# Latent attention of a macaron block: masked maxima on VectorE, scores by key tile, one query projection per pair, values in four runs

## Chip, cores and metric

One core of a Trainium2 chip runs the whole program. The metric is the device time of one execution in microseconds (us), the median of the runs. Engines: TensorE (PE for its matmuls, PEld for its weight loads), VectorE (DVE), ScalarE (ACT), GpSimd (POOL) and SyncE (SP), which here only issues DMAs.

## The reference

The program is a chain of six residual steps on x of shape (4, 1024, 128): a routed feed-forward step, an attention with a polynomial in place of softmax, the routed step again, a feed-forward step, the latent attention, and the feed-forward step again. The change touches only the latent attention:

```python
Wdkv = x @ latent_w + latent_b                       # (4, 1024, 36): keys and values of all heads
q = einsum('btc,hcl->bhtl', x, Wd_w) + Wd_b          # 16 heads of 36
scores = einsum('bhtl,bsl->bhts', q, Wdkv) / sqrt(8)
scores = where(causal, scores, -inf)
y = einsum('bhts,bsl->bhtl', softmax(scores), Wdkv)
out = y.transpose(0, 2, 1, 3).reshape(b, t, 16 * 36) @ out_w + out_b
```

## The kernel before

The latent attention is `attn1_phase`. It works batch by batch (4), and in each batch through 8 pairs of heads; pair m has the heads c = 0 and 1. Each engine has its own instruction stream, built from `start`, `pair` and `finish` by `pipeline`, and the streams meet at semaphores. A pair's work is spread over three rounds of the loop: in the round of pair m, TensorE computes the transposed scores and the values of pair m, the row maxima of pair m+1, and the query projection of pair m+2.

- **Queries.** `project(m, c)` multiplies the normalised input by the projection of head c. Precision is kept by splitting each float32 number into a high and a low part of type fp32r and adding three products, so it is three matmuls of 512 columns for each half sequence. The weights hold each head's 36 columns three times over, so that 108 rows come out; ScalarE (`low_query`, line 1795) and VectorE (`query`, line 1904) make rows high, high, low out of them and write them into qS.
- **Maxima.** `scores_max(m, q, v, keys)` takes tile v of 16 (head v // 8, query tile j = v % 8), multiplies 128 queries by the (j + 1) * 128 keys before them, and adds the causal mask of the last 128 columns by one more matmul of a bf16 identity and a bf16 mask (line 1642). VectorE's `maximum` takes the row maximum (line 1910). Two PSUM regions alternate, so tile v waits for the maximum of tile v - 2. `transpose_max`, `high_max` and `low_max` turn the 16 columns of maxima into rows, and four DMAs (`maxima` on SP, lines 1536 and 1537) put them into rows 108 and 109 of qS, where they are subtracted inside the score product.
- **Transposed scores.** `scores(m, q, u)` works through ten units: per half sequence a diagonal unit of four tiles of 128 x 128 and a mask matmul of 512 columns (line 1659), a unit of 384 and 128 columns, one of 256, and for the second half four full units of 512. Unit u of a head waits until ScalarE's exponential (line 1820) has read unit u - 1 from the same PSUM bank. The exponentials go to probs, which has two slots.
- **Values.** `values(m, q, u)` (line 1671) multiplies probs by V in plain float32. Head 0 goes to partitions 0 to 63 and head 1 to partitions 64 to 127, so these matmuls use half-width tiles of the array. The values of unit u - 1 follow the scores of unit u.
- **What goes where.** `MAXIMA` says how many maxima tiles follow the scores of each unit: all 16 are spread over units 0 to 6. After unit 8 comes `transpose_max`, after that the projection of head 0 of pair m+2, after unit 9 that of head 1. Pair 6 of a batch also opens the next batch (`opens`), and after pair 7 comes `finish`, the output product.

Of the kernel before, what the change touches and what calls it, by code (L numbers as in the profile page):

```python
# [34 lines left out]
def after(n):  # L35

    return n + 1 + LEAD
# [1378 lines left out]
PAIRS = HEADS // 2  # L1416
STACK = 3 * LAT
KROWS = STACK + 2
ZW = 5 * P
VW = 64  # L1420
L1_COLS = 2 * LAT + 8 + 4 * HEADS


def key_units(s):
# [6 lines left out]
    return [diagonal, split, half] + [[(i, 0, 0, HALF, False)] for i in range(k)]  # L1431


def attn1_phase(nc, t, tag):
# [8 lines left out]
    with ExitStack() as ctx:  # L1443
        def sb(name, shape, dt=F32):
# [5 lines left out]
        wd = [sb(f"wd{i}", [P, HEADS * STACK], F32R) for i in range(2)]  # L1450
        lat = [sb(f"lat{i}", [P, STACK], F32R) for i in range(2)]
        v_bias, k_bias, k_low, q_low = cols[:, 0:LAT], cols[0:STACK, 36:37], cols[0:STACK, 37:38], cols[0:STACK, 38:39]
        q_bias = cols[0:STACK, 40:40 + HEADS]
        k_lbias = sb("k_lbias", [STACK, 1])
        qb_low = sb("qb_low", [STACK, HEADS])
# [8 lines left out]
        wcur = sb("wcur", [P, 2, 2 * STACK], F32R)  # L1464
        bcur = sb("bcur", [STACK, 2, 2])
        qT = sb("qT", [STACK, 2, HALF], F32R)
# [4 lines left out]
        probs = sb("probs", [P, 2, 2, HALF])  # L1471
# [3 lines left out]
        zT = sb("zT", [P, 2, ZW])  # L1475
        res = ResidualAdd(ctx, nc, sem, t, tag, 1)
# [5 lines left out]

        k_in, w_high, w_low, rstd_ready = sem("k_in"), sem("w_high"), sem("w_low"), sem("rstd_ready")
        minus = sb("minus", [2, SEQ], F32R)
        const_ready, minus_ready = sem("const_ready"), sem("minus_ready")
# [3 lines left out]
        wq_ready, qp_ready, qt_ready, qs_ready = sem("wq_ready"), sem("qp_ready"), sem("qt_ready"), sem("qs_ready")  # L1489
        sm_ready, mx_ready, mt_ready, mh_ready, ml_ready, m_in = (  # L1490
            sem("sm_ready"), sem("mx_ready"), sem("mt_ready"), sem("mh_ready"), sem("ml_ready"), sem("m_in"))
        s_ready, p_ready, pv_ready, y_ready, yc_ready = (
            sem("s_ready"), sem("p_ready"), sem("pv_ready"), sem("y_ready"), sem("yc_ready"))
# [4 lines left out]
        units = [(s, u) for s in range(2) for u in key_units(s)]  # L1498
        NU = len(units)
        NQ0 = len(key_units(0))  # L1500
        PRODUCTS = ((0, 0), (1, 0), (0, 1))

        def pipeline(eng, start, pair, finish):


            def element(b, more):
                with eng.Fori(0, PAIRS // 2 - 1) as i:
                    for q in range(2):
                        pair(b * PAIRS + i * 2 + q, q, i * 2 + q, b, (True, True))
# [14 lines left out]
        MAXIMA = (range(0, 4), range(4, 6), range(6, 7), range(7, 9), range(9, 12), range(12, 14), range(14, 16))  # L1524

        with nc.Block() as block:
            @block.sync
            def _(sp):
# [9 lines left out]

                def pair(m, q, i, b, ahead):
                    if ahead[0]:  # L1540
                        maxima(m + 1, 1 - q)

                pipeline(sp, lambda: maxima(0, 0), pair, lambda b, more: None)
# [536 lines left out]
```

## Time and profile before

| | |
|---|---|
| median of 3 runs | 3431.35 us (3430.93 to 3438.45) |
| span of the profiled execution | 3431.1 us |
| PE, DVE, ACT busy over the span | 89%, 66%, 38% |
| latent attention, from and to | about 2280 us to 3325 us |
| one pair in the steady part | 26.3 to 27.0 us |
| all four batches, 32 pairs | about 1045 us |

The profiled execution's own time is its span. A busy share counts an instruction from its first to its last cycle, also while the next one already runs. The column of the granted clock tells at which of its two levels, 1.2 and 2.4 GHz, TensorE ran: 1.00 is 2.4 GHz.

### The profile page before, as it was taken

The numbers are of one execution on the slowest core, as the hardware profiler recorded it, in microseconds if no ns is written. First come the engines' busy times: TensorE is split into PE (matmuls) and PEld (weight loads), VectorE is DVE, ScalarE is ACT, GpSimd is POOL, SyncE is SP. The second block draws the span as 40 slices with busy tenths as digits, with TensorE's granted clock in tenths as the row PEclk, the third lists the DMA queues.
The fourth block names the chain that finished last, engine by engine and source line by source line (L and its number), as shares of the span: only waits on it lengthen the run. The fifth ranks groups of instructions, "written<-read, shape, count | busy, mean of one in ns | idle before, by whom it ended". The sixth has DMA issues, their size and how long they took to land. (4 is left out here: it accounts for less than half of the span.)

```text
span 3431.1 us, 60614 instructions
## 1 busy us (share of the span) xinstructions
PE 3037.7 (89%) x18088; PEld 2189.2 (64%) x18088; DVE 2268.8 (66%) x5128; ACT 1317.9 (38%) x2660; POOL 765.6 (22%) x1073
## 2 busy tenths in 40 slices
PE   5999999787777877769999999779989989999987
PEld 4777777565555555547777777446666666666653
DVE  6777777587786877857777777345555555555533
ACT  2111111266665765641111111225545545545532
POOL 1323232154354444422323232000000000000000
PEclk9999999888998888979999999779999999999998
DMA  3000000000000000011000000000000000000000
GB/s 121 0 0 0 0 0 0 1 2 2 3 3 3 2 2 2 2 63 35 0 0 0 0 0 0 1 0 1 1 2 1 1 2 1 1 2 1 1 1 25
DMA packets 13037, 24.17 MB, mean 7 GB/s; under 512 B 2306, under 2 KB 7682, under 8 KB 12804
## 3 DMA queue, kind: packets, MB, share of 16 engines
q1 hardware_dynamic: 12804, 21.22, 1.9%
q8 instruction: 127, 2.08, 0.3%
q14 instruction: 106, 0.87, 0.1%
HBM read 18.52 MB, written 2.10 MB: 6 GB/s over the span
## 5 line engine op out<-in xcount | busy, mean ns | idle before, releaser
L555 DVE SCALAR_TENSOR_TENSOR moe_acc<-moe_ps,moe_comb,moe_acc 128x512 f32<-128x512 f32 x896 | 661.7, 745 | 174.0 <-PE moe_ps L304 170.9
L1335 DVE SCALAR_TENSOR_TENSOR attn_R<-attn_R 128x512 f32<-128x512 f32 (+1 forms) x592 | 478.5, 864 | 115.5 <-ACT attn_R L1221 115.1
L1910 DVE TENSOR_REDUCE attn_mx<-attn_psm 128x1 f32<-128x128 f32 (+7 forms) x512 | 369.3, 754 | 243.0 <-PE attn_psm L1642 242.4
L1820 ACT ACTIVATE attn_probs<-attn_pse 128x512 f32<-128x512 f32 (+1 forms) x640 | 323.4, 553 | 330.1 <-PE attn_pse L1655 263.6
L304 PE MATMUL moe_ps<-moe_Wg,moe_xh 128*128 128x512 f32 x1024 | 328.8, 403 | 24.2 <-DVE moe_Wu L501 24.2
L1221 ACT ACTIVATE attn_R<-attn_ps 128x512 f32<-128x512 f32 (+1 forms) x640 | 321.2, 568 | 64.9 <-PE attn_ps L1079 64.8
L335 PE MATMUL moe_ps<-moe_Wd,moe_ih 128*128 128x512 f32 x1024 | 338.0, 411 | 0.0
L304 PE MATMUL moe_ps<-moe_Wu,moe_xh 128*128 128x512 f32 x1024 | 337.1, 411 | 0.0
L1671 PE MATMUL attn_psy<-attn_probs,attn_V 128*64 128x128 f32 (+3 forms) x2304 | 317.7, 397 | 0.1
L1079 PE MATMUL attn_ps<-attn_qS,attn_kM 128*128 128x128 f32 (+3 forms) x1152 | 263.9, 372 | 45.9 <-issue 43.2
L1079 PEld LDWEIGHTS attn_ps<-attn_qS,attn_kM 128*128 128x128 f32 x1152 | 210.1, 228 | 109.9 <-issue 60.0
L1655 PE MATMUL attn_pse<-attn_qS,attn_kS 110*128 110x128 f32 (+3 forms) x1152 | 261.2, 341 | 13.0 <-issue 9.7
L1098 PE MATMUL attn_ps<-attn_R,attn_KV 128*32 128x128 f32 (+3 forms) x2304 | 171.4, 412 | 110.3 <-DVE attn_R L1335 110.2
L454 POOL TENSOR_SCALAR moe_part<-consts,moe_pick,moe_prob 128x8 f32<-128x8 f32 x256 | 98.2, 398 | 755.8 <-ACT moe_prob L389 755.8
L1655 PEld LDWEIGHTS attn_pse<-attn_qS,attn_kS 110*128 110x128 f32 x1152 | 172.7, 194 | 121.3 <-issue 83.4
L1023 POOL TENSOR_TENSOR attn_L<-attn_L,attn_small 128x512 f32<-128x512 f32 x128 | 206.7, 1646 | 163.5 <-ACT attn_L L1220 163.5
L304 PEld LDWEIGHTS moe_ps<-moe_Wg,moe_xh 128*128 128x128 f32 x1024 | 194.5, 191 | 73.9 <-issue 28.0
L1639 PE MATMUL attn_psm<-attn_kS,attn_qS 108*128 108x512 f32 (+3 forms) x672 | 212.0, 402 | 14.3 <-DVE attn_mx L1910 10.7
L388 ACT ACTIVATE moe_prob<-moe_gap 128x2 f32<-128x2 f32 x64 | 13.1, 204 | 548.6 <-DVE moe_gap L546 548.6
L335 PEld LDWEIGHTS moe_ps<-moe_Wd,moe_ih 128*128 128x128 f32 x1024 | 186.0, 191 | 41.7 <-issue 1.1
L304 PEld LDWEIGHTS moe_ps<-moe_Wu,moe_xh 128*128 128x128 f32 x1024 | 187.2, 192 | 36.8
L1561 POOL CAST attn_wcur<-attn_wd 128x216 fp32r (+1 forms) x64 | 21.5, 365 | 828.8 <-DVE attn_qS L1904 822.9
(207 smaller groups left out, 5302.4 us busy)
## 6 DMA issues: line engine op xcount, KB each, us to landing
moe_stageg<-in_w_gate SPq DMA_DIRECT2D x8, 512.0 KB, 6.8
moe_stageu<-in_w_up SPq DMA_DIRECT2D x8, 512.0 KB, 7.5
moe_stageg<-in_w_down SPq DMA_DIRECT2D x8, 512.0 KB, 3.6
out<-X SPq DMA_DIRECT2D x1, 2048.0 KB, 8.7
attn_qS<-attn_mh SPq DMA_DIRECT2D x64, 4.0 KB
attn_qS<-attn_ml SPq DMA_DIRECT2D x64, 4.0 KB
attn_wd<-in_wd SPq DMA_DIRECT2D x1, 864.0 KB, 5.5
attn_w<-in_wqkv SPq DMA_DIRECT2D x1, 768.0 KB, 5.1
```

Source lines behind the costliest of these rows:

```text
L304: last = pe.matmul(expert_bank[j % 4][:, :], a[q][:, :], w[b][:, cols], start=k == 0, stop=k == 2)
L335: last = pe.matmul(y_bank[h][:, :], a[q][:, rows], W[2][b][:, cols], start=c == 0 and k == 0, stop=c == KC - 1 and k == 2)
L555: dve.scalar_tensor_tensor(acc[:, q, r, :], expert_bank[j % 4][:, :], comb[:, q, r, e:e + 1], acc[:, q, r, :], ALU.mult, ALU.add).then_inc ...
L1023: pool.tensor_tensor(L[:, s, j, :], L[:, s, j, :], seen, ALU.mult).then_inc(g_ready, 1)
L1079: last = pe.matmul(e_bank[j][:, at_:at_ + n], kM[q][:, j, kt * P:(kt + 1) * P], qS[q][:, s * HALF + qc:s * HALF + qc + n], start=not diago ...
L1221: act.activation(R[:, u % 2, j, HALF - n:HALF], e_bank[j][:, HALF - n:HALF], ACT.Relu).then_inc(r_ready, 1)
L1335: dve.scalar_tensor_tensor(r, r, -SLOPE, r, ALU.add, ALU.mult).then_inc(u_ready, 1)
L1639: pe.matmul(m_all[:, base + lo:base + hi], qS[q][c][0:STACK, j * P:(j + 1) * P], keys[0:STACK, lo:hi], start=True, stop=hi < (j + 1) * P)
L1655: last = pe.matmul(e_bank[c][:, at_:at_ + n], kS[:, kt * P:(kt + 1) * P], qS[q][c][:, s * HALF + qc:s * HALF + qc + n], start=True if not ...
L1671: last = pe.matmul(y_bank[VW * c:VW * (c + 1), qc:qc + n], V[:, kt, :], probs[:, u % 2, c, at_:at_ + n], start=first and k == 0, stop=end, ...
L1820: act.activation(probs[:, u % 2, c, HALF - n:HALF], e_bank[c][:, HALF - n:HALF], ACT.Exp, scale=SCORE_SCALE).then_inc(p_ready, 1)
L1910: dve.reduce_max(mx[:, q, v:v + 1], m_all[:, base:base + (v % 8 + 1) * P], AX.X).then_inc(mx_ready, 1)
```

## The change

Four things change in the latent attention.

- **Masked maxima.** The mask matmul of each maxima tile goes. VectorE holds a float32 tile `causal` (896 zeros and the mask) and uses one `tensor_tensor_reduce` in place of `reduce_max`: it adds `causal` to the scores, writes the sum to `masked` and the maximum to mx. Before it stands a wait on the tile before the last.
- **Scores by key tile.** The diagonal units are cut by key tile: 512 columns with a mask of 128, 384 and 128 columns with a mask of 256, 256 columns with a mask of 128.
- **One projection.** `project(m)` computes both heads at once, 72 rows, six matmuls a pair. ScalarE makes the high part qh, VectorE the low part ql, and SP copies the rows to their places in qS by six DMAs of 36 rows x 4 KB (`query_rows`). The maxima of that pair wait for these DMAs. They are issued behind the four DMAs of `maxima`.
- **Four runs of values.** probs has five slots, and the values of a pair come in four runs: units 0 to 2 after unit 3, units 3 to 5 after unit 6, units 6 and 7 after unit 8, and units 8 and 9 after unit 0 of the next pair. MAXIMA moves with them: none at unit 0, three in a row at units 2, 4, 5 and 7, the last at unit 7. The first two pairs of a batch are written out before the loop.

```diff
+RING = 5
+PAIR = 2 * LAT
+def tile_units(s):
+    k = 4 * s
+    return [[(k, 0, 0, HALF, True)], [(k + 1, P, P, 3 * P, True), (k + 3, 0, 3 * P, P, True)],
+            [(k + 2, 2 * P, 2 * P, 2 * P, True)]] + [[(i, 0, 0, HALF, False)] for i in range(k)]
...
-        probs = sb("probs", [P, 2, 2, HALF])
+        probs = sb("probs", [P, RING, 2, HALF])
+        causal = sb("causal", [P, SEQ])
+        masked = sb("masked", [P, 2, SEQ])
+        TOGETHER = ((0, 1, 2), (3, 4, 5), (6, 7), (8, 9))
+        AFTER = {3: 0, 6: 1, 8: 2}
...
-        MAXIMA = (range(0, 4), range(4, 6), range(6, 7), range(7, 9), range(9, 12), range(12, 14), range(14, 16))
+        MAXIMA = ((), range(0, 2), range(2, 5), range(5, 6), range(6, 9), range(9, 12), range(12, 13), range(13, 16))
...
+                def query_rows(m, q):
+                    sp.wait_ge(ql_ready, after(m * 2 + 1))
+                    sp.wait_ge(s_ready, after((m - 1) * 2 * NU - 1))
+                    for c in range(2):
+                        for k, part in enumerate((qh, qh, ql)):
+                            sp.dma_start(f32(qS[q][c][k * LAT:(k + 1) * LAT, :]),
+                                         f32(part[c * LAT:(c + 1) * LAT, :])).then_inc(q_in, 16)
...
-                def project(m, c):
+                def project(m):
...
-                            last = pe.matmul(m_bank[2 * c + s][0:STACK, :], wcur[:, w, c * STACK:(c + 1) * STACK],
+                            last = pe.matmul(m_bank[s][0:PAIR, :], wcur[:, w, :],
                                              xT[a][:, s * HALF:(s + 1) * HALF], start=k == 0, stop=k == 2)
...
                 def scores_max(m, q, v, keys):
+                    if v == 0:
+                        pe.wait_ge(q_in, (m + 1) * ROWS_IN)
...
-                    pe.matmul(m_all[:, base + j * P:base + (j + 1) * P], t.identb, t.neg_qk, start=False, stop=True).then_inc(sm_ready, 1)
...
                     for u in range(NU):
                         scores(m, q, u)
+                        if u == 0 and not first_pair:
+                            values(m - 1, NG - 1)
...
-                        if u >= 1:
-                            values(m, q, u - 1)
+                        if u in AFTER:
+                            values(m, AFTER[u])
...
+                def high_query(m):
+                    for s in range(2):
+                        act.wait_ge(qp_ready, after(m * 2 + s))
+                        if s == 0 and not (isinstance(m, int) and m == 0):
+                            act.wait_ge(q_in, m * ROWS_IN)
+                        act.activation(qh[:, s * HALF:(s + 1) * HALF], m_bank[s][0:PAIR, :], ACT.Identity,
+                                       bias=bcur[:, :]).then_inc(qh_ready, 1)
...
+                def low_query(m):
+                    for s in range(2):
+                        half = slice(s * HALF, (s + 1) * HALF)
+                        dve.wait_ge(qh_ready, after(m * 2 + s))
+                        dve.scalar_tensor_tensor(ql[:, half], m_bank[s][0:PAIR, :], bcur[:, :], f32(qh[:, half]),
+                                                 ALU.add, ALU.subtract).then_inc(ql_ready, 1)
...
                     dve.wait_ge(sm_ready, after(m * 16 + v))
-                    base = (v % 2) * 2 * HALF
-                    dve.reduce_max(mx[:, q, v:v + 1], m_all[:, base:base + (v % 8 + 1) * P], AX.X).then_inc(mx_ready, 1)
+                    dve.wait_ge(mx_ready, after(m * 16 + v - 2))
+                    dve.sem_inc(max_pause, 1)
+                    base, n = (v % 2) * 2 * HALF, (v % 8 + 1) * P
+                    dve.tensor_tensor_reduce(masked[:, v % 2, 0:n], m_all[:, base:base + n], causal[:, SEQ - n:SEQ], 1.0, NEG,
+                                             ALU.add, ALU.max, mx[:, q, v:v + 1]).then_inc(mx_ready, 1)
```

## Rows read from the trace of the kernel before

**Rows 1.** The page, busy time by engine and the granted clock in 40 slices

```profile
PE 3037.7 (89%) x18088; PEld 2189.2 (64%) x18088; DVE 2268.8 (66%) x5128; ACT 1317.9 (38%) x2660; POOL 765.6 (22%) x1073
...
PEclk9999999888998888979999999779999999999998
```

**Rows 2.** Busy time by stretch: us, PE, PEld, DVE, ACT, POOL, clock, DMA, GB/s

```profile
12.00:14.00 2.00, 0.00 (x0) 0.00 (x0) 1.84 (x10) 0.00 (x0) 0.00 (x0) 1.00 1.03 410
2302.00:2306.00 4.00, 2.76 (x13) 1.78 (x14) 3.40 (x7) 0.00 (x0) 2.27 (x6) 1.00 0.01 2
2306.00:2310.00 4.00, 2.61 (x13) 1.43 (x12) 3.65 (x6) 0.00 (x0) 0.00 (x0) 0.99 0.00 0
2310.00:2314.00 4.00, 3.96 (x12) 2.36 (x13) 2.98 (x5) 0.00 (x0) 0.00 (x0) 0.50 0.00 0
2321.00:2530.00 209.00, 204.09 (x1303) 128.67 (x1302) 116.76 (x176) 111.55 (x211) 7.39 (x32) 1.00 0.00 1
```

**Rows 3.** SP's timeline, a first load, and first DMAs of `maxima` in two pairs

```profile
8.41 0.43 SPq L267 DMA_DIRECT2D moe_stageg<-in_w_gate  x1
...
2344.06 0.64 SPq L1536 DMA_DIRECT2D attn_qS<-attn_mh  x1
2344.75 0.64 SPq L1537 DMA_DIRECT2D attn_qS<-attn_ml  x1
...
2477.41 0.63 SPq L1536 DMA_DIRECT2D attn_qS<-attn_mh  x1
```

**Rows 4.** Groups by line and shape in the latent attention, mean ns behind busy us

```profile
L1910 DVE TENSOR_REDUCE attn_mx<-attn_psm 128x1 f32<-128x1024 f32 x64 | 78.1, 1220 | 60.0 <-PE attn_psm L1642 60.0
L1910 DVE TENSOR_REDUCE attn_mx<-attn_psm 128x1 f32<-128x512 f32 x64 | 44.0, 687 | 7.6 <-PE attn_psm L1642 7.3
L1904 DVE SCALAR_TENSOR_TENSOR attn_qS<-attn_psm,attn_bcur,attn_qT 108x512 fp32r<-108x512 f32 x128 | 91.1, 749 | 76.0 <-PE attn_pse L1655 46.5 <-ACT attn_qT L1795 29.3
L1876 DVE TENSOR_TENSOR attn_xT<-attn_psm,attn_xT 128x512 fp32r<-128x512 f32 x8 | 5.2, 688 | 1.7 <-ACT attn_xT L1774 1.6
L1335 DVE SCALAR_TENSOR_TENSOR attn_R<-attn_R 128x512 f32<-128x512 f32 x464 | 433.3, 989 | 115.5 <-ACT attn_R L1221 115.1
L1795 ACT ACTIVATE attn_qT<-attn_psm,attn_bcur,attn_small 108x512 fp32r<-108x512 f32 x122 | 89.6, 785 | 40.7 <-PE attn_psm L1626 40.2 <-DVE attn_qS L1904 0.5
L1820 ACT ACTIVATE attn_probs<-attn_pse 128x512 f32<-128x512 f32 x512 | 281.2, 596 | 215.4 <-PE attn_pse L1655 148.9 <-PE attn_pse L1659 63.9
```

**Rows 5.** Timeline of a steady pair: weight loads and matmuls where kinds of work meet

```profile
2396.90 1.20 PEld L1626 LDWEIGHTS attn_psm<-attn_xT,attn_wcur 128*108 128x108 f32 x6 [0.81 <-issue]
2398.15 0.42 PEld L1655 LDWEIGHTS attn_pse<-attn_qS,attn_kS 110*128 110x128 f32 x2
...
2402.19 0.52 PEld L1655 LDWEIGHTS attn_pse<-attn_qS,attn_kS 110*128 110x128 f32 x4 [0.81 <-issue]
2403.33 0.20 PEld L1639 LDWEIGHTS attn_psm<-attn_kS,attn_qS 108*128 108x128 f32 x1
...
2420.06 0.72 PE L1655 MATMUL attn_pse<-attn_qS,attn_kS 110*128 110x512 f32 x2
2420.67 1.08 ACT L1820 ACTIVATE attn_probs<-attn_pse 128x512 f32<-128x512 f32 x2 [1.22 <-PE attn_pse L1655]
2420.71 1.08 PE L1671 MATMUL attn_psy<-attn_probs,attn_V 128*64 128x512 f32 x4
2421.72 0.73 PE L1655 MATMUL attn_pse<-attn_qS,attn_kS 110*128 110x512 f32 x2
```

**Rows 6.** Timeline of the last batch: the last DMA of `maxima` and who waits

```profile
3266.22 0.64 SPq L1537 DMA_DIRECT2D attn_qS<-attn_ml  x1
...
3268.03 0.66 PE L1655 MATMUL attn_pse<-attn_qS,attn_kS 110*128 110x128 f32 x4 [1.42 <-DMA attn_qS<-attn_ml]
```

**Rows 7.** Timeline of the end of one steady pair, from maxima to row DMAs

```profile
2422.29 0.27 PE L1647 MATMUL attn_pso<-consts,attn_mx 128*16 128x128 f32 x1
...
2423.59 0.28 DVE L1914 TENSOR_TENSOR attn_ml<-attn_pso,attn_mh 16x128 fp32r<-16x128 f32 x1 [2.37 <-ACT attn_mh L1800]
```

More of the change, by code:

```diff
@@ L1496, in attn1_phase @@
         kc_ready, act_pause, pool_pause = sem("kc_ready"), sem("act_pause"), sem("pool_pause")
-        units = [(s, u) for s in range(2) for u in key_units(s)]
+        units = [(s, u) for s in range(2) for u in tile_units(s)]
         NU = len(units)
-        NQ0 = len(key_units(0))
+        NQ0 = len(tile_units(0))
         PRODUCTS = ((0, 0), (1, 0), (0, 1))
@@ L1506, in element @@
             def element(b, more):
-                with eng.Fori(0, PAIRS // 2 - 1) as i:
+                for i in range(2):
+                    pair(b * PAIRS + i, i, i, b, (True, True))
+                with eng.Fori(1, PAIRS // 2 - 1) as i:
                     for q in range(2):
@@ L1541, in pair @@
                         maxima(m + 1, 1 - q)
-                pipeline(sp, lambda: maxima(0, 0), pair, lambda b, more: None)
+                    if ahead[1]:
+                        query_rows(m + 2, q)
+                pipeline(sp, start, pair, lambda b, more: None)
             @block.gpsimd
@@ L1655, in scores @@
                             last = pe.matmul(e_bank[c][:, at_:at_ + n], kS[:, kt * P:(kt + 1) * P],
-                                             qS[q][c][:, s * HALF + qc:s * HALF + qc + n], start=True if not diagonal else k == 0,
+                                             qS[q][c][:, s * HALF + qc:s * HALF + qc + n], start=k == 0,
                                              stop=not diagonal, skip_group_check=diagonal)
                         if diagonal:
-                            last = pe.matmul(e_bank[c][:, :], t.identb, t.neg_kq, start=False, stop=True, skip_group_check=True)
+                            lo, hi = min(p[1] for p in pieces), max(p[1] for p in pieces) + P
@@ L1677, in start @@
                     latents(0)
+                    pe.wait_ge(xl_ready, after(1))
+                    project(0)
                     latent_rows(0)
-                    for c in range(2):
-                        project(0, c)
                     for v in range(16):
@@ L1891, in start @@
                     next_keys(0)
-                    for g in range(4):
-                        query(0, 0, g)
+                    low_query(0)
                     for v in range(16):
@@ L1929, in pair @@
                     if ahead[1]:
-                        for g in range(4):
-                            query(m + 2, q, g)
+                        low_query(m + 2)
                 def finish(b, more):
```

159 lines of the change are left out of this document (76 added, 83 removed).

## The prediction

> **What bounds the kernel now.** I read the page first: TensorE is the busiest engine of the whole program [rows 1]. The change touches only the latent attention, so the next view is the busy time by stretch. In 2321 to 2530 us TensorE shows 204.09 of 209 us at a granted clock of 1.00, VectorE 117 and ScalarE 112 [rows 2]. The reader is to see that the other two are a little over half full, and that nothing is said yet of whether their work lies in the right place. SP's timeline gives the length of a pair: from 2344.06 to 2477.41 are five pairs, 26.67 us each [rows 3]. Then the groups for the price of one operation [rows 4], and the timeline for what happens where two kinds of work meet [rows 5, 6, 7].
>
> **Prices.** Six projection matmuls of 512 columns take 1.25 us from first to next load, so 512 fp32r columns cost 0.21 us, one column a cycle at 2.4 GHz. Four tiles of 128 columns need four weight loads in 0.52 us: a load that nothing hides costs 0.125. Values: the scores of one unit start at 2420.06 (load 0.125, stream 0.43, end 2420.61), the values at 2420.71, the next scores load at 2421.72. From 2420.61 to that unit's first column at 2421.85 are 1.24 us, of which the four value matmuls stream 4 x 0.213 = 0.85. So going into half-width tiles and out again costs 0.38 us [rows 5]. VectorE's maximum costs 154 ns and 1.04 ns a column (687 at 512, 1220 at 1024); successive ones are taken to overlap by 0.07 [rows 4]. Two exponentials take 1.08 us [rows 5].
>
> **TensorE's savings, per pair.**
> - 16 mask matmuls of the maxima: 128 columns (0.053) and the 0.072 us of the next weight load that so short a matmul doesn't hide, 0.125 each: 2.0 us.
> - Projection, 12 matmuls to 6: 6 x 0.213 = 1.3 us.
> - Values: nine runs become four (the last two units already lie together), 5 x 0.36 (0.38 less a little that the masks beside them share): 1.8 us. Their columns stay the same.
> - Scores by key tile: a diagonal unit took 1.14 us (2402.19 to 2403.33) and now takes two times 512 + 128 columns with one open load, about 0.63. The 384/128 unit gains a mask of 256 columns a head and the 256 unit one of 128, with loads in part hidden: 0.12 and 0.2 us. Net 0.2 a half sequence, 0.4 us a pair.
>
> Sum 5.5 us. If TensorE's own work were all, a pair would fall by a fifth, and 27 to 30 such pairs by some 160 us.
>
> **Why I don't book that.** I laid both orders out by hand over a pair: each engine's instructions in program order, each as early as the prices and its waits allow. For the kernel before this gives 24.9 us of TensorE work and 1.2 us of waits, 26.1 us a pair against 26.67 measured; its landmarks stay close to the trace (unit 7 starts 17.7 us behind unit 0 and unit 8 19.3; in the trace 2420.06 - 2402.19 = 17.9 and 19.5 [rows 5]). The new order gives 19.3 us of work and 9.7 us of waits, 29.05 us a pair. The waits, in the pair's time (unit 0 at 0):
>
> 1. *Rows of the queries, 2.4 us.* The copies start only when the projection has passed through ScalarE and VectorE. Unit 8's `transpose_max` is visible at 24.2; then values of units 6 and 7 (to 26.1) and the projection (to 27.4); ScalarE makes two high halves (0.69 each: 785 ns with bias and scale pointers before, 596 for an exponential without them, the middle taken), VectorE the second low half (749 ns [rows 4]): low rows ready at 29.3. SP then issues six DMAs at 0.675 us each (2344.06 to 2344.75 [rows 3]). A DMA of 4 KB was awaited until 1.81 us after its issue began [rows 6]; 147 KB at the 410 GB/s of the first loads [rows 2] adds 0.4 to 0.5, so I take 2.3. The last row lands 0.675 x 5 + 2.3 = 5.7 us later, at 35.0, which is 5.9 us into the next pair. There, unit 0's scores, the held-over values (2.1 us) and unit 1's scores are through by 3.5, and maxima tile 0 stands in front of everything else in TensorE's queue. SP's four DMAs of `maxima` (issued 24.9 to 27.6) are past by then and don't delay the six.
> 2. *Maxima three in a row, 4.3 us.* Only two regions exist, so the third of each group waits for VectorE to finish the first: 0.9 at tiles 2 to 4, 2.4 at tiles 8 to 11, 1.0 at tile 15. Between the groups VectorE has nothing, because TensorE is in 2.1 us of values. Before, the maxima started at unit 0 with a value run of 1 us between groups, and these waits were 1.2 us.
> 3. *`transpose_max`, 1.4 us.* The last maximum (1.22 us) now follows unit 7, and only unit 8's scores cover it. Before, it followed unit 6 with a value run and two units of scores behind it.
> 4. *Unit 0 of the next pair, 1.6 us.* It needs unit 9's exponential, which stands in ScalarE's queue behind the two high halves, and these wait for the projection. Before, the values of units 8 and 9 filled this place.
>
> The four DMAs of the maxima rows (ml in [rows 7], then 4 x 0.675 + 1.8) land at about 28.7, just ahead of unit 0: if ScalarE were quicker, this wait would take over.
>
> So a pair costs 29.05 - 26.1 = 2.95 us more.
>
> **Bounds of what the trace doesn't show.** *The masked maximum:* a TENSOR_TENSOR from PSUM costs 688 ns at 512 columns, the reduction 687 [rows 4], so I take it at the same price. Above stands line 1335's 989 ns at 512, 0.3 us more, which gives 31.6 us a pair. Below, at half a cycle a column, 26.6; nothing in PSUM-reading float32 rows goes that fast. *The copies:* an issue of 0.43 us, as for a large load early in the program [rows 3], gives 27.8; copies that land before anyone needs them 27.4; a landing of 3.6 us 30.35. So no end of the copies' price brings the pair under 26.1.
>
> A rule of the Trainium skill speaks on the masked maximum: the page Vector Engine (DVE) Microarchitecture Reference, section Points that are easy to get wrong, says that such an instruction with two SBUF sources wider than bf16 and an accumulator runs at half its rate. Here one source lies in PSUM, so by its words it doesn't apply; if it did, rival C below would be the forecast. No row of before shows a fused maximum.
>
> **Sum over the run.** Twenty steady intervals (pairs 1 to 5 of four batches): +59. Pair 0 of each batch has neither held-over values nor a wait for rows (they were copied before `finish`): 29.05 - 2.4 - 2.1 = 24.6, -1.5 x 4 = -6. The opening pairs save two value runs and six matmuls behind unit 8 but wait longer for rows: +1 x 3. The last pair of three batches ends with its values behind the late exponential: +6.7 x 3 = +20. In the last batch pair 6 keeps waits 1 to 3 (+2), pair 7 has only scores and values (-2). The start trades one projection for six DMAs: 0. The smaller weight copies save 1 to 2, the mask tile gives 1 back. Together +75 on the profiled execution's 3431.1; the median is 3431.35, so **about 3506 us**.
>
> **The rivals.**
> - *A, faster: the chain between two pairs is covered.* Waits 1, 3 and 4 (5.4 us) form one chain from the last maximum to the next pair's first. If it ran beside TensorE's work, only the waits for VectorE would stay: 23.7 us, 2.4 less than 26.1, over 27 pairs -65: 3366 us. It decides from 3 us of that chain gone. For it: 5.5 us of work truly goes, and VectorE and ScalarE have room. Against: each link is in queue order in the code. Chance 0.17.
> - *B, TensorE's clock.* At the start of the phase, with maxima alone, TensorE was busy 2.76 and 2.61 of 4 us, and the clock then went from 1.00 to 0.50 [rows 2]. In the new order the stretch from 3.5 to 10 us of each pair has 2.4 + 0.9 us of waits in 6.5, a similar share. If the clock falls there, the value run of 2.1 us takes 4.2; over 27 pairs some 60 to 75 us more, 3565 to 3580. Chance 0.2.
> - *C, the masked maximum runs at half rate.* Twice the columns' time gives 35.0 us a pair, +5.9 x 27 = +160 on the forecast: 3665 us. With 0.3 us more an instruction, +2.6 x 27 = +70: 3576. Chance 0.08 for both, mostly the latter.
> - *D, no change:* the waits come to the 5.5 us that the work loses. Chance 0.05.
> - The forecast itself, 3440 to 3560 (its lower end is the quick issue, 1.2 us a pair less; its upper end the slow landing and a little of B): 0.5.
>
> **Numbers.** Within 0.3% (10 us) is what a measurement can't tell from no change. Faster 0.17, same 0.05, slower 0.78. The range is 3405 to 3640: it leaves out the lower half of A and the far end of C.
>
> **What would show it.** Right: SP's first maxima DMA comes every 29 us in the steady part; line 1642 is gone; TensorE's idle time names the row DMAs at the first maxima tile (2.4 us a pair), the masked maximum at the third of a group, and the last maximum before `transpose_max`; its busy share in the steady part falls from 98% to some 75%. Wrong: if the rows land before 3.5 us into the pair, step 1 goes; if six row DMAs issue in under 0.5 us each, half of it; if the masked maximum shows much above 1.22 us at 1024 columns, C; if the granted clock shows under 1.00 in steady pairs, B; if a steady pair is under 26 us, the whole layout of waits was wrong, and A is right.

## The result and the profile after

The changed kernel takes 3754.4 us (median of 4 runs, 3751.3 to 3760.9) against 3431.1 before. The ratio is 1.0939, 95% interval 1.0918 to 1.0961. The profiled execution has a span of 3749.5 us. So it is 323 us slower. I had forecast 75 us slower, and a range that ended at 3640.

The page, busy time and granted clock; they answer to [rows 1].

```profile
PE 3079.9 (82%) x16488; PEld 2117.4 (56%) x16488; DVE 2232.1 (60%) x5577; ACT 1264.7 (34%) x2590; POOL 754.2 (20%) x1041
...
PEclk9999999799888898799999986878887878798888
```

TensorE has 1600 matmuls fewer, and is busy 42 us longer. A matmul's duration grows at the lower clock, and the last 16 slices of the clock show mostly 7 and 8 where there were nearly all nines. The busy time by stretch says the same of the steady part [rows 2]; below it are stretches of 2 us of one pair.

```profile
2321.00:2530.00 209.00, 156.61 (x628) 81.23 (x627) 72.35 (x190) 70.81 (x138) 3.35 (x18) 0.79 0.09 26
```

```profile
2400.00:2402.00 2.00, 1.63 (x10) 0.71 (x6) 0.00 (x0) 1.04 (x3) 0.00 (x0) 1.00 0.58 158
2402.00:2404.00 2.00, 0.00 (x0) 0.00 (x0) 0.00 (x0) 0.54 (x2) 0.00 (x0) 1.00 0.48 141
2404.00:2406.00 2.00, 0.00 (x0) 0.00 (x0) 0.00 (x0) 0.00 (x0) 0.00 (x0) 0.72 0.28 98
2406.00:2408.00 2.00, 1.91 (x8) 1.72 (x8) 0.73 (x4) 0.67 (x2) 0.00 (x0) 0.50 0.00 0
...
2412.00:2414.00 2.00, 2.00 (x6) 0.63 (x8) 0.97 (x2) 0.00 (x0) 0.00 (x0) 0.50 0.00 0
2414.00:2416.00 2.00, 2.00 (x13) 0.95 (x10) 0.00 (x0) 0.00 (x0) 0.00 (x0) 0.72 0.00 0
...
2426.00:2428.00 2.00, 1.21 (x4) 0.67 (x4) 2.00 (x5) 0.32 (x1) 0.00 (x0) 1.00 0.00 0
2428.00:2430.00 2.00, 1.09 (x3) 0.38 (x5) 1.06 (x3) 1.03 (x3) 0.00 (x0) 0.69 0.00 0
2430.00:2432.00 2.00, 2.00 (x8) 0.47 (x4) 0.00 (x0) 0.00 (x0) 0.00 (x0) 0.50 0.02 4
```

For 4 us, 2402 to 2406, TensorE does nothing while the DMA moves 141 and 98 GB/s. The clock falls to 0.50 (1.2 GHz) within that wait (0.72 in its last 2 us) and stays there for some 9 us of the work behind it. It falls a second time between 2428 and 2430, in the second of two thin stretches (TensorE busy 1.21 and 1.09 of 2 us). SP's timeline shows why TensorE stands still [rows 3].

```profile
2392.25 0.66 SPq L1556 DMA_DIRECT2D attn_qS<-attn_mh  x1
...
2398.20 1.52 SPq L1565 DMA_DIRECT2D attn_qS<-attn_qh  x2
2399.76 0.71 SPq L1565 DMA_DIRECT2D attn_qS<-attn_ql  x1
2400.52 2.32 SPq L1565 DMA_DIRECT2D attn_qS<-attn_qh  x2
2402.89 0.71 SPq L1565 DMA_DIRECT2D attn_qS<-attn_ql  x1
2429.93 0.66 SPq L1556 DMA_DIRECT2D attn_qS<-attn_mh  x1
```

A pair lasts 2429.93 - 2392.25 = 37.7 us; it was 26.67, and I had laid out 29.05. The row copies begin at 2398.20, the last one at 2402.89. TensorE's timeline of the same pair (in brackets the idle time before, and who ended it), with one row of VectorE:

```profile
2406.09 0.79 PE L1676 MATMUL attn_psm<-attn_kS,attn_qS 108*128 108x128 f32 x2 [4.46 <-DMA attn_qS<-attn_ql]
...
2411.86 3.97 PE L1710 MATMUL attn_psy<-attn_probs,attn_V 128*64 128x512 f32 x16
...
2418.53 0.33 PE L1676 MATMUL attn_psm<-attn_kS,attn_qS 108*128 108x128 f32 x1 [0.91 <-DVE attn_mx L1949]
...
2421.96 2.37 PE L1710 MATMUL attn_psy<-attn_probs,attn_V 128*64 128x512 f32 x16
...
2428.91 0.38 PE L1683 MATMUL attn_pso<-consts,attn_mx 128*16 128x128 f32 x1 [1.11 <-DVE attn_mx L1949]
2429.22 3.39 PE L1710 MATMUL attn_psy<-attn_probs,attn_V 128*64 128x512 f32 x8
...
2435.42 0.50 PE L1691 MATMUL attn_pse<-attn_qS,attn_kS 110*128 110x512 f32 x1 [0.80 <-ACT attn_probs L1856]
```

```profile
2417.38 1.09 DVE L1949 CUSTOM_DVE_ANT_0 attn_masked<-attn_psm,attn_causal 128x896 f32<-128x896 f32 x1 [4.26 <-PE attn_psm L1676]
```

Sixteen value matmuls of the same shapes take 3.97 us mostly at the half clock and 2.37 at the full one. While they run TensorE makes no new tile: VectorE finishes the one that stood ready and is then idle for 4.26 us. And the groups by shape, beside [rows 4]:

```profile
L1949 DVE CUSTOM_DVE_ANT_0 attn_masked<-attn_psm,attn_causal 128x1024 f32<-128x1024 f32 x10 | 12.2, 1222 | 0.0
...
L1949 DVE CUSTOM_DVE_ANT_0 attn_masked<-attn_psm,attn_causal 128x512 f32<-128x512 f32 x11 | 7.6, 690 | 1.5 <-PE attn_psm L1676 1.5
L1949 DVE DVE_READ_ACCUMULATOR2_ANT attn_mx<- 128x1 f32 x86 | 7.2, 83 | 0.0
```

The masked maximum costs what the reduction did (1222 and 690 ns against 1220 and 687), but each drags a second instruction of 83 ns behind it.

### The profile page after: what moved, and what is told of

The parts are those of the page before. It is cut to its first block and busy times, and to the rows that moved or that the text cites. A ratio compares the mean times of both kernels' runs of the same rounds, so it can differ in the third digit from the quotient of the medians.

```text
span 3749.5 us, 57897 instructions
## 1 busy us (share of the span) xinstructions
PE 3079.9 (82%) x16488; PEld 2117.4 (56%) x16488; DVE 2232.1 (60%) x5577; ACT 1264.7 (34%) x2590; POOL 754.2 (20%) x1041
## 5 line engine op out<-in xcount | busy, mean ns | idle before, releaser
L1949 DVE CUSTOM_DVE_ANT_0 attn_masked<-attn_psm,attn_causal 128x128 f32<-128x128 f32 (+7 forms) x512 | 375.7, 757 | 608.7 <-PE attn_psm L1676 603.8
L1676 PE MATMUL attn_psm<-attn_kS,attn_qS 108*128 108x512 f32 (+3 forms) x672 | 241.3, 454 | 194.7 <-DMA attn_qS<-attn_ql 108.0
L1710 PE MATMUL attn_psy<-attn_probs,attn_V 128*64 128x512 f32 (+3 forms) x1536 | 370.9, 630 | 0.8 <-ACT attn_probs L1856 0.8
L1691 PE MATMUL attn_pse<-attn_qS,attn_kS 110*128 110x512 f32 (+3 forms) x768 | 269.2, 430 | 38.3 <-ACT attn_probs L1856 25.4
L1676 PEld LDWEIGHTS attn_psm<-attn_kS,attn_qS 108*128 108x128 f32 x672 | 140.7, 235 | 258.2 <-DVE attn_mx L1949 135.9
L1597 POOL CAST attn_wcur<-attn_wd 128x72 fp32r<-128x72 f32 (+1 forms) x64 | 13.9, 247 | 1096.3 <-DVE attn_ql L1941 1090.5
L1691 PEld LDWEIGHTS attn_pse<-attn_qS,attn_kS 110*128 110x128 f32 x768 | 156.4, 221 | 119.5 <-issue 70.0
L1710 PEld LDWEIGHTS attn_psy<-attn_probs,attn_V 128*64 128x64 f32 x1536 | 119.0, 172 | 184.4 <-issue 151.5
```

The lines of the kernel that those rows point to most:

```text
L1676: last = pe.matmul(m_all[:, base + lo:base + hi], qS[q][c][0:STACK, j * P:(j + 1) * P], keys[0:STACK, lo:hi], start=True, stop=True)
L1691: last = pe.matmul(e_bank[c][:, at_:at_ + n], kS[:, kt * P:(kt + 1) * P], qS[q][c][:, s * HALF + qc:s * HALF + qc + n], start=k == 0, stop ...
L1710: last = pe.matmul(y_bank[VW * c:VW * (c + 1), qc:qc + n], V[:, kt, :], probs[:, u % RING, c, at_:at_ + n], start=first and k == 0, stop=e ...
L1949: dve.tensor_tensor_reduce(masked[:, v % 2, 0:n], m_all[:, base:base + n], causal[:, SEQ - n:SEQ], 1.0, NEG, ALU.add, ALU.max, mx[:, q, v: ...
```

## The experiments

Each run is given as a ratio to the kernel before, measured beside it; "+130 us" is (ratio - 1) x 3431. First, which part of the change costs, put together and taken apart.

**e1: the change with the projection of before** (two heads' projections, rows straight into qS, no row copies).

```diff
-                    for c in range(2):
-                        for k, part in enumerate((qh, qh, ql)):
-                            sp.dma_start(f32(qS[q][c][k * LAT:(k + 1) * LAT, :]), ...
+                for c in range(2):
+                    project(m, c)
```

> The changed kernel with the projection of before (12 matmuls a pair, rows written by ScalarE and VectorE, no row DMAs); masked maxima, key tiles, four runs and the new MAXIMA stay. Theory R (the wait for the row DMAs and the fall of the clock that follows it cost most of the 11 us a pair): no TensorE idle of over 2 us, granted clock near 1.00 in steady pairs, a pair of 27.5 to 29 us, 3450 to 3500 us. Rival V (the waits for VectorE between three maxima in a row and the long value runs thin TensorE's work out and bring the clock down by themselves): the clock still falls in each pair, 31 us a pair or more, over 3560 us.

3564.5 us, ratio 1.0378 (1.0349 to 1.0407), +130. It fits neither range: 192 us go with the new projection, and 130 stay. In its trace the clock still falls up to twice a pair, among the maxima and value runs, with no row copies there:

```profile
2394.00:2396.00 2.00, 2.00 (x6) 0.64 (x7) 0.97 (x2) 0.50 (x1) 0.00 (x0) 0.50 0.00 0
...
2404.00:2406.00 2.00, 2.00 (x6) 0.65 (x7) 0.89 (x4) 0.69 (x2) 0.00 (x0) 0.50 0.00 0
```

The pair around these two stretches lasts 33.3 us, the one before it, whose clock falls only at its very end, 28.6. So the late order loses the clock by itself, here 4.7 us in a pair.

**e3: the new projection alone** on the kernel before: `project(m)`, `high_query`, `low_query`, `query_rows`, and nothing else.

> The kernel before with the new projection and its row DMAs alone. Theory R: the first maxima stand right behind unit 0's scores here, so TensorE waits some 4 us a pair for the rows, the clock falls behind it, and 1.3 us of matmuls are saved: a pair of 32 to 35 us, 3580 to 3680 us. Rival V: the row wait costs only itself, 29 to 30 us a pair, 3500 to 3530 us.

3647.9 us, ratio 1.0620 (1.0591 to 1.0649), +213. Its waiting tile, with the clock of the same stretch:

```profile
2396.23 0.47 PE L1660 MATMUL attn_psm<-attn_kS,attn_qS 108*128 108x128 f32 x1 [5.14 <-DMA attn_qS<-attn_ql]
```

```profile
2391.00:2393.00 2.00, 0.09 (x1) 0.00 (x0) 0.00 (x0) 1.94 (x3) 0.00 (x0) 0.98 0.58 158
2393.00:2395.00 2.00, 0.00 (x0) 0.00 (x0) 0.00 (x0) 0.00 (x0) 0.00 (x0) 0.50 0.51 162
...
2401.00:2403.00 2.00, 2.00 (x19) 1.72 (x17) 1.39 (x2) 0.00 (x0) 0.00 (x0) 0.50 0.00 0
```

TensorE waits for the row copies 29 times in this kernel, 160.6 us in total. One part of four, tried alone, costs two thirds of the whole loss.

**e4: the masked maxima alone** on the kernel before.

```diff
-                    dve.reduce_max(mx[:, q, v:v + 1], m_all[:, base:base + (v % 8 + 1) * P], AX.X).then_inc(mx_ready, 1)
+                    dve.tensor_tensor_reduce(masked[:, v % 2, 0:n], m_all[:, base:base + n], causal[:, SEQ - n:SEQ], 1.0, NEG,
+                                             ALU.add, ALU.max, mx[:, q, v:v + 1]).then_inc(mx_ready, 1)
```

> The kernel before with the masked maxima alone. TensorE loses 16 mask matmuls a pair (2.0 us by the hand layout), VectorE gains 0.08 us an instruction (1.3 us), and it is no bound here: a pair of 24.9 to 25.7 us, 3385 to 3410 us under both theories. If the mask matmuls were hidden anyway: 3431 us.

3438.3 us, ratio 1.0014 (0.9999 to 1.0030). The 2 us a pair that TensorE was spared bring nothing, though I had expected 3385 to 3410 us under both theories. The run changes two things at once: VectorE also has the 16 accumulator reads more.

**e5 and e6: masks and key tiles, in the early and in the late order of the maxima.** e5 adds `tile_units` to e4; e6 is e5 with one line more:

```diff
-        MAXIMA = (range(0, 4), range(4, 6), range(6, 7), range(7, 9), range(9, 12), range(12, 14), range(14, 16))
+        MAXIMA = ((), range(0, 2), range(2, 5), range(5, 6), range(6, 9), range(9, 12), range(12, 13), range(13, 16))
```

> The kernel before with the masked maxima and the transposed scores by key tile, and nothing else of the change: ten value runs a pair, the order of the maxima of before, the old projection. TensorE has 2.4 us a pair less to do (16 masks of 0.125 and 0.4 of the scores). If TensorE's own work sets the pair, 32 pairs give 3355 to 3385 us. If the chain from one maximum to the next sets it (a maximum, the accumulator read of 0.08 us behind it, the next scores), both savings only lengthen TensorE's waits: 3425 to 3445 us.

> As the last one, with the order of the maxima of after (none behind unit 0, three in a row behind units 2, 4, 5 and 7), still ten value runs a pair. Theory O (the late order with three in a row thins TensorE's work, and the granted clock falls): 3500 to 3570 us, near the 3564 of the kernel that has this order, the four runs and the old projection. Theory G (the grouped value runs starve the chain of maxima, since only two tiles of scores can stand ready, and the order alone costs a wait of 0.5 to 1 us a pair): 3430 to 3470 us, with a clock above 0.93.

e5: 3424.6 us, ratio 0.9963 (0.9945 to 0.9980), -13, as the chain of maxima would have it. e6: 3525.2 us, ratio 1.0243 (1.0219 to 1.0266), +83. The order alone costs 96 us, with ten value runs a pair. Theory O is right, and G, that the order hurts only through joined runs, falls. But under the late order joining them costs too: e1, the same with four runs, stands at 1.0378, 46 us above e6. Three neighbouring pairs of e6 with the same instructions:

```profile
2347.11:2375.42 28.31, 25.00 (x122) 12.75 (x121) 14.92 (x37) 13.81 (x27) 0.92 (x4) 1.00 0.01 2
2375.42:2417.04 41.62, 37.89 (x122) 18.54 (x121) 14.93 (x37) 15.70 (x28) 0.92 (x4) 0.63 0.00 0
2417.04:2445.67 28.63, 25.26 (x122) 12.98 (x121) 14.92 (x37) 13.82 (x27) 0.92 (x4) 1.00 0.00 1
```

The late order has two prices. At the full clock e6's pairs alternate in three of the four batches between some 28.5 and 30.1 us, where e5's last mostly 26.0 and 26.5: about 3 us a pair. And in this execution two pairs last 41.6 and the change to the last batch 71.7 in place of 61.6, with the clock down; beside pairs of 30.1 that is some 33 us. So about a third of the 96 us is the clock, and most of the rest is waiting.

**e7: the change with the projection and the order of before** (masked maxima, key tiles, four value runs).

> Masked maxima, key tiles and four value runs, with the order of the maxima of before and the old projection. Theory G: a value run of 2 to 3 us leaves VectorE idle for 1 to 2 us four times a pair, so the order does not save it: 3500 to 3580 us. Theory O: with the early order the five restarts of 0.36 us that the grouping spares come through at least in part: 3370 to 3430 us.

3426.9 us, ratio 0.9973 (0.9961 to 0.9984), -9. With the early order the four runs do no harm, and no good either (e5 is the same with ten runs; the intervals overlap). A steady pair lasts 26.9 us, no less than the 26.67 of before. One of its value runs, and VectorE's next maximum:

```profile
2407.31 2.37 PE L1690 MATMUL attn_psy<-attn_probs,attn_V 128*64 128x512 f32 x16
```

```profile
2410.95 0.42 DVE L1938 CUSTOM_DVE_ANT_0 attn_masked<-attn_psm,attn_causal 128x256 f32<-128x256 f32 x1 [2.41 <-PE attn_psm L1656]
```

**e11: the whole change in the early order** (the `MAXIMA` line of before).

> The whole change with the order of the maxima of before (four tiles behind unit 0). The late order cost 137 us with the old projection (3564 against 3427). If it costs as much under the new one: 3600 to 3640 us, below the 3648 of the new projection alone. If the rows' wait, which comes at the same instant of the pair in both orders, absorbs part of it, since the later tiles have nothing to wait for before the rows are there: 3660 to 3700. If the early tiles hold up the scores of unit 1 and with them the whole pair: 3740 or more.

3633.3 us, ratio 1.0579 (1.0540 to 1.0618), +199. This closes the square: -9 with neither cost (e7), +130 with the late order (e1), +199 with the new projection (e11), +322 with both. The projection and its copies cost 208 us in one order and 192 in the other; the order costs 139 under one projection and 123 under the other. They nearly add up. The projection's share can be set against the row waits of the changed kernel's trace:

```profile
PE attn_psm L1676 <- DMA attn_qS<-attn_ql: 132.1, 29, 9.7
```

(Us in total, how many waits, the longest one.) 132 of some 200 us are the waits themselves; e2 below speaks on the rest.

**What the row copies cost.** Four variants of the changed kernel.

*e8*: the copies of head 0 and head 1 are counted on two semaphores, and the first eight tiles wait for the first alone.

```diff
-                    if v == 0:
-                        pe.wait_ge(q_in, (m + 1) * ROWS_IN)
+                    if j == 0:
+                        pe.wait_ge(q_in[c], (m + 1) * ROWS_IN)
```

> The kernel after, with the six row copies counted on two semaphores, so that the first eight tiles of maxima wait for the three copies of the first head alone. The last of those three is issued about 3.1 us ahead of the last of the six, so the first tile of maxima starts some 3 us earlier in each pair. If the rows' wait costs what it lasts: 3 us by 30 pairs, 3750 less 90, 3650 to 3675 us. If it also costs TensorE its clock in the stretch behind it, and the shorter wait (2 us in place of 5) keeps it up: 3580 to 3640. If the second head's maxima then find their rows late, which they should not, since they come some 8 us later, no gain: 3740 or more.

3689.4 us, ratio 1.0729 (1.0702 to 1.0757), 72 less than the change. From the first copy's issue to tile 0 it is 2403.66 - 2397.78 = 5.9 us, 2.0 less than in the changed kernel (2406.09 - 2398.20 = 7.9) and not 3: the second head's copies follow on the same queue, and head 0's last one was there only 4.3 us after its issue began. None of the three expectations holds: the wait shrinks by less than 3 us, and the clock still falls in the pair.

*e9*: six copies of half the columns (the edit below, with n = 512). *e10*: twelve of half the columns, two for each of the six.

```diff
-                            sp.dma_start(f32(qS[q][c][k * LAT:(k + 1) * LAT, :]),
-                                         f32(part[c * LAT:(c + 1) * LAT, :])).then_inc(q_in, 16)
+                            sp.dma_start(f32(qS[q][c][k * LAT:(k + 1) * LAT, 0:n]),
+                                         f32(part[c * LAT:(c + 1) * LAT, 0:n])).then_inc(q_in, 16)
```

> The kernel after with six row copies of half the queries each (columns 0 to 511, from the third pair on; the other half keeps the rows of an older pair, so the scores of those queries are not this pair's). The number of copies and their order on the queue stay. Theory N (the number of copies sets when the last one lands: six issues of 0.77 us and a fixed time behind them): no change, 3735 to 3770 us. Theory S (their size sets it: 0.86 MB a pair at 160 GB/s is 5.4 us, which is what passes from the first issue's end to the wait's end): half the bytes take 2 to 2.7 us less a pair, 60 to 80 us less, and what the clock then gives back comes on top: 3640 to 3695 us.

> The kernel after with the same bytes in twelve copies of half the columns. Theory N: six more issues of 0.7 us a pair, 4.2 us by 30 pairs on the path, 3860 to 3900 us. Theory S: the queue keeps the bytes flowing at the same rate while it issues; 12 issues of 0.7 are 8.4 us, longer than the 5.4 us of the bytes, so the issues now decide and half of the 4.2 us shows: 3800 to 3850 us. Unchanged (3740 to 3770) if a small copy's issue is much cheaper than 0.7 us.

e9: 3704.8 us, ratio 1.0780 (1.0741 to 1.0819), 54 less than the change. e10: 3845.6 us, ratio 1.1189 (1.1149 to 1.1230), 86 more. e9's copies and its tile 0:

```profile
2399.63 1.52 SPq L1566 DMA_DIRECT2D attn_qS<-attn_qh  x2
2401.19 0.71 SPq L1566 DMA_DIRECT2D attn_qS<-attn_ql  x1
2401.94 1.47 SPq L1566 DMA_DIRECT2D attn_qS<-attn_qh  x2
2403.46 0.71 SPq L1566 DMA_DIRECT2D attn_qS<-attn_ql  x1
```

```profile
2405.85 0.79 PE L1677 MATMUL attn_psm<-attn_kS,attn_qS 108*128 108x128 f32 x2 [2.77 <-DMA attn_qS<-attn_ql]
```

Half-size copies issue every 0.77 us (3.83 from the first to the last) and the last is there 2.39 us later: 6.2 us. At full size one issue of the six is held up, 2.32 for two where e9 has 1.47, so that first to last takes 4.69, and the last needs 3.20: 7.9 us. So five steps from issue to issue make 3.8 us, the arrival of a half-size copy 2.4, and the second half of the bytes 1.7; what the first half's bytes take isn't shown apart. In e10 a first copy is issued at 2413.93 and tile 0 starts at 2424.70, 10.8 us, 4.6 more than in e9 for six more issues. So the count of copies is the larger part, and the size is real, but here smaller than the 2 us of theory S. e9 fell between the two theories. e10 fell into the range of theory S, which had the issues decide once there are twelve; but the 5.4 us that S puts between the first issue's end and the wait's end are some 7.1.

The waits for rows over the whole execution, for e9, e8 and e10:

```profile
PE attn_psm L1677 <- DMA attn_qS<-attn_ql: 91.4, 29, 9.8
PE attn_psm L1676 <- DMA attn_qS<-attn_ql: 77.7, 29, 7.8
PE attn_psm L1678 <- DMA attn_qS<-attn_ql: 223.0, 29, 12.6
```

Against 132.1 in the changed kernel, e9 waits 41 us less and is 54 faster, e8 54 less and 72 faster, e10 91 more and 86 slower. A shorter wait gave back somewhat more than its length, a longer one cost no more than its length.

*e2*: ahead of the wait for the rows, 36 matmuls of 256 columns that feed nothing.

```diff
+                            if u == WARM_AT and not last_pair:
+                                for _ in range(36):
+                                    pe.matmul(o_bank[:, 256:512], t.identb, t.neg_kq[:, 0:256], start=True, stop=True)
```

> The changed kernel with 36 matmuls of 256 columns (3.8 us at full clock) whose result nobody reads, put after unit 1's scores, in front of the wait for the row DMAs, in pairs 0 to 6 of each batch. Theory R: they lie inside a wait of 4.5 us, so they delay nothing where the rows are late, and keep the clock at 1.00 behind it: the maxima and value run behind the wait lose some 4 us, a pair goes from 37.7 to some 33.5 us, about 3640 us. Rival V: the clock falls a little later all the same; the time stays within 1% of 3754 us or rises.

3693.0 us, ratio 1.0740 (1.0708 to 1.0771), 68 less than the change, with more work. Tile 0 starts just as late behind the first copy (2402.92 - 2395.14 = 7.8 us), so what is won isn't the wait but the clock behind it: at least 68 us of the rows' price. The clock is held up only for a while, as rival V had it:

```profile
2403.00:2405.00 2.00, 1.79 (x8) 1.00 (x8) 1.20 (x5) 0.66 (x2) 0.00 (x0) 1.00 0.03 8
...
2407.00:2409.00 2.00, 2.00 (x6) 0.62 (x7) 0.97 (x2) 0.48 (x1) 0.00 (x0) 0.50 0.00 0
...
2417.00:2419.00 2.00, 2.00 (x7) 0.68 (x7) 0.91 (x4) 0.71 (x2) 0.00 (x0) 0.50 0.00 0
```

Behind tile 0 it shows 1.00, and then it falls twice, as in e1, where there is no such wait. So the time lies between theory R's 3640 us and rival V's 3716.

**e12: the late order (e6) with fillers** of 256 columns, four or five ahead of the third tile of each group of three.

```diff
+FILL = {4: 4, 8: 4, 11: 5, 15: 5}
...
+                                for _ in range(FILL.get(v, 0)):
+                                    pe.matmul(o_bank[:, 256:512], t.identb, t.neg_kq[:, 0:256], start=True, stop=True)
```

> The kernel with masked maxima, key tiles and the late order (3525 us), with 18 matmuls of 256 columns a pair that feed nothing, four or five ahead of the third tile of each group of three, where TensorE waits 0.6 to 0.9 us for VectorE. They last about 0.5 us a place at 2.4 GHz, so the waits cover them. If TensorE's thin stretches are what lowers the granted clock, it stays at 1.00 and each pair lasts 28.6 us, as the pairs at full clock do there: 3480 to 3500 us. If the clock falls for another reason, 3525 us and more, since at half clock the fillers are longer than the waits.

3504.9 us, ratio 1.0198 (1.0161 to 1.0236), against 1.0243 for e6. The intervals of the two ratios overlap a little, though the times don't (3502 to 3509 and 3513 to 3531). The pair that lasted 41.6 us in e6:

```profile
2376.55:2407.78 31.23, 28.59 (x141) 15.17 (x140) 14.93 (x37) 15.29 (x28) 0.92 (x4) 0.95 0.00 1
```

It lasts 31.2 us at 0.95. The time is just above the range of the first theory (3480 to 3500): no pair of 41.6 is left, but every second pair of most batches lasts 31.2 to 32.7 where e6 has 30.1. That speaks for the thin stretches as a cause of the clock's fall.

**Where TensorE's savings went.** e7 has all of the masks', key tiles' and four runs' savings, 4.2 us a pair by my count, and gains 0.3 (9 us by 32). Three variants of e7.

*e13*: each maximum over the first half of its columns, and the exponential's scale divided by 1024. *e14*: the mask matmul and the plain reduction of before. *e15*: only the last two groups of values joined.

```diff
+                    lo, n = SEQ - n, n // 2
-                                             scale=SCORE_SCALE).then_inc(p_ready, 1)
+                                             scale=SCORE_SCALE / 1024).then_inc(p_ready, 1)
```

```diff
-        TOGETHER = ((0, 1, 2), (3, 4, 5), (6, 7), (8, 9))
-        AFTER = {3: 0, 6: 1, 8: 2}
+        TOGETHER = ((0,), (1,), (2,), (3,), (4,), (5,), (6, 7), (8, 9))
+        AFTER = {1: 0, 2: 1, 3: 2, 4: 3, 5: 4, 6: 5, 8: 6}
```

> Masked maxima, key tiles, four value runs and the early order (3427 us), with each maximum over the first half of its columns alone and the exponential's scale divided by 1024 (so the maxima and the outputs are not the reference's; instructions and their number stay). VectorE has some 5 us a pair less to do. Theory V (the chain from maximum to maximum through VectorE took up what TensorE was spared): the pair falls from 26.9 us towards TensorE's own 24.7, 3360 to 3385 us. Theory T (TensorE's own work and restarts set the pair): 3420 to 3430 us.

> The same kernel (3427 us) with the maxima of before: a mask on TensorE for each tile and a plain reduction, so no accumulator read of 0.08 us on VectorE. Key tiles, four runs and the early order stay. Theory V: the masks take time in which TensorE waits for VectorE anyway, and 16 reads of 0.08 leave the chain: 3400 to 3440 us. Theory T: 16 masks of 0.125 us by 32 pairs come on top: 3470 to 3490 us.

> The same kernel (3427 us) with the value runs of units 0 to 5 apart again and only those of units 6, 7 and 8, 9 joined, behind most of the maxima. Theory V: a long value run costs when tiles of maxima are still to come, since VectorE has two tiles at most ahead and idles 2.4 us in a run of 2.4; single runs are covered, and the two restarts spared at the pair's end come through, 0.72 us by 32 pairs off the 3424 of ten runs: 3395 to 3410 us. If the pair's end waits for the last maximum and not for TensorE, nothing: 3418 to 3430 us.

e13: 3370.7 us, ratio 0.9816 (0.9795 to 0.9836), -63. Same instructions, less of VectorE's time, and a part of the savings appears (a pair lasts 25.3 us in place of 26.9): VectorE's maxima were on the path. e14: 3414.8 us, ratio 0.9944 (0.9923 to 0.9966), -19. Sixteen masks a pair came back on TensorE and cost nothing; the ratio is below e7's, though its interval still overlaps that one's (0.9961 to 0.9984) a little. e15: 3428.9 us, ratio 0.9981 (0.9970 to 0.9992): no gain over e7, so the joined runs' starving of VectorE isn't what eats the gain either. e14 has the lowest ratio of the kernels that compute the reference, though its interval overlaps with that of e5: key tiles and four value runs, with the masks, the projection and the order of before.

## Why the prediction was wrong

**The failed step is the sum of the waits: the clock was left out of it, which is the larger part, and wait 1 was mis-sized.** The direction, the code's chain and the places of the waits were right. The steady pair was laid out at 29.05 us and lasts 37.7, 8.6 more. By landmarks of the pair whose unit 0 starts at 2397.80 (the next one's is the row at 2435.42):

- *Up to maxima tile 0:* laid out 5.9 us, measured 2406.09 - 2397.80 = 8.3, +2.4. This is wait 1, the rows: booked at 2.4 us, it lasts 4.46. I had taken 0.675 us an issue (the rows gave 0.69) and 2.3 for the landing. It was 0.77 an issue, one held up, and 3.2 for a full-size copy. My 2.3 holds for the half-size copy of e9 (2.39). The transfer's rate came from the first loads of the program [rows 2], 410 GB/s, by which 147 KB take 0.36 us and not the 0.4 to 0.5 that I added; the stretches with row copies show 140 to 160. The Trainium skill, page DMA: Bandwidth & Descriptors, section Anatomy of one DMA (on the software path), fits 2.0 us and the bytes at 436 GB/s for a DMA issued by GpSimd, by which an estimate for 147 KB is 2.3 us; here SP issues, the full-size copy took 3.20, and the measurement decides.
- *From tile 0 to `transpose_max`:* laid out 18.3, measured 2428.91 - 2406.09 = 22.8, +4.5. The first value run is 3.97 in place of 2.37, and the maxima and scores ahead of it, 2406.09 to 2411.86, take 5.8 in place of the 3.6 of my layout; both lie mostly where the clock shows 0.50. In e2, where the clock stays up for the first part of that stretch, it takes 2407.52 - 2402.92 = 4.6. The other 0.7 I put down to the accumulator reads, 16 of 83 ns, half of them hidden; that is what is left over and not shown apart.
- *From `transpose_max` to the next unit 0:* laid out 4.85, measured 6.5, +1.7. The run of units 6 and 7 takes 3.39 in place of 1.94, again at 0.50.

So of 8.6 us the clock made about 5.2, an estimate (1.6 and 2.2 ahead of `transpose_max`, 1.4 behind it), the rows 2.4 and the reads perhaps 0.7. In e1, two falls make a pair 4.7 us longer, which is of that size.

**Rival B**, with a chance of 0.2, was the mechanism of the larger part: the stretch from 3.5 us on is thin, and the clock falls. I called the thinness similar to that of the start of the phase. It wasn't: there TensorE was busy 2.76 and 2.61 of 4 us, 69% and 65% [rows 2], and by my own layout 3.2 of 6.5, 49%. The layout should have had the clock in its sum. B's price, 60 to 75 us over 27 pairs, was half of 5.2 x 27 = 140. I had priced one value run; the maxima and scores ahead of it slow down too, and it falls a second time, in the thin stretch around waits 2 and 3. For the rows' wait e2 shows the clock's share by itself (68 us). The first fall lies in the same wait that was 2.4 us too short. The clock's 140 us would have taken 3506 to 3646, just past the range's end; all 8.6 us over 27 pairs make 232, so 3738; the last 16 us I didn't take apart.

**Wait 2**, three maxima in a row, is there (0.91 and 0.83 us rows, VectorE idle up to 4.3 us; TensorE's waits for maxima in this pair sum to 2.9 us where 4.3 were laid out), and e6, e7 and e11 show that it comes from the order: 96 us with ten value runs, 123 and 139 with four. The layout had about 3.1 us a pair, 84 us over 27 pairs, and that is what e6 shows against e5 at the full clock (about 3 us). What the layout lacked was again the clock.

**Wait 3** was laid out at 1.4 and measured 1.11. **Wait 4** was laid out at 1.6; behind a slower unit 9 the row at 2435.42 shows 0.80. The busy share of TensorE, forecast at 75%, is 156.61 of 209, 75%: right for another reason, since a slower clock counts as busy.

**The savings on TensorE**, 5.5 us a pair, were booked as work and are worth little; no run shows whether the count itself is right, since even e13 brings out only 1.6 of 4.2 us. The kernel before was said to have 24.9 us of TensorE work and 1.2 of waits; I read that as TensorE setting its pace. e4, e13 and e14 show that the maxima through VectorE are nearly as long a chain: take 2 us of masks from TensorE and nothing happens, put them back and nothing is lost, take half the columns from VectorE and 54 us go. VectorE stood at 117 of 209 us [rows 2], and I said myself that this tells nothing of where the work lies; I then took its waits in the kernel before for 1.2 us and no limit.

**The masked maximum** (rival C) has the reduction's price, so the Trainium skill's rule on two SBUF sources didn't apply, as its words say; the 690 ns row agrees. What I missed is the second instruction. The Trainium skill, page VectorE: DVE Perf Modes, section Two Vector instructions with no wait between them, says that an operation that writes out its accumulator counts as two, itself and an accumulator read; the trace agrees, 512 reads of 83 ns.

Open stays why the clock, once down in e6, kept at 0.50 for 28 us, why ScalarE let TensorE wait 1.9 us ahead of it, and why it fell there and not elsewhere. Ahead of the fall TensorE was busy 1.32 and 0.77 of two stretches of 2 us; two pairs later, from 2450 to 2454, it was busy 1.59 and 0.50, the same sum, and the clock stayed at 1.00. So a thin stretch came before each fall that I looked at, but not a fall behind each thin stretch. That the rows could be copied earlier, with a third buffer for qS, was not tried.

## What to carry to other kernels

A wait on the busiest engine costs what it lasts and can then cost what the clock takes: price the work behind it at half speed, up to where the trace shows the clock back, and look for every thin stretch of the loop, not only the first. Before you count a saving on one engine, draw the chain through the engine that it alternates with; a mask that moves from a matmul onto a reduction is a saving only if the reduction isn't on that chain. Moving data between partitions by many small DMAs costs an issue each, one after another, so copies that the next step waits for have to be few and early.

## What the runs showed of the hardware that was not expected

- Copies of 36 rows x 4 KB inside SBUF: mostly 0.76 us from issue to issue, about 1.6 once in each six, the last one there 3.2 us after its issue began, 141 to 158 GB/s with a DMA share of 0.48 to 0.58; of 36 rows x 2 KB: 0.77 and 2.39 us.
- Three pairs of the same instructions in one execution of e6: 28.3, 41.6 and 28.6 us, at granted clocks of 1.00, 0.63 and 1.00. The fall, the rise, and two stretches in a later pair in which TensorE was as thin and the clock stayed:

```profile
2380.00:2382.00 2.00, 1.32 (x8) 0.49 (x4) 0.72 (x2) 1.31 (x2) 0.92 (x4) 1.00 0.00 0
2382.00:2384.00 2.00, 0.77 (x4) 0.68 (x5) 0.00 (x0) 1.68 (x4) 0.00 (x0) 1.00 0.00 0
2384.00:2386.00 2.00, 2.00 (x9) 0.54 (x8) 0.73 (x4) 1.06 (x2) 0.00 (x0) 0.71 0.00 0
...
2414.00:2416.00 2.00, 2.00 (x7) 0.84 (x7) 0.10 (x2) 0.52 (x2) 0.00 (x0) 0.61 0.00 0
...
2450.00:2452.00 2.00, 1.59 (x8) 0.49 (x4) 0.98 (x2) 1.24 (x3) 0.75 (x4) 1.00 0.00 0
2452.00:2454.00 2.00, 0.50 (x4) 0.41 (x4) 0.00 (x0) 1.92 (x3) 0.17 (x2) 1.00 0.00 0
```

- The fused maximum with a mask in SBUF runs at the rate of the plain reduction (1222 against 1220 ns at 1024 columns), plus 83 ns.
